# Layer 1's attention: preparation and routing laid out unit by unit, scatters in even units

## The reference

```python
x = x + tanh(g_xattn[0]) * L0_xattn(layernorm(x), ctx)          # 8 heads of 64
x = x + tanh(g_ffn[0])   * L0_ffn(layernorm(x))                 # top 2 of 8, silu(a)*b
x = x + tanh(g_xattn[1]) * L1_xattn(layernorm(x), ctx, ctx)     # 16 heads of 8, biases
x = x + tanh(g_ffn[1])   * L1_ffn(layernorm(x))                 # top 2 of 8, gelu
```

```python
qh, kh, vh = proj(q, Wq, bq), proj(k, Wk, bk), proj(v, Wv, bv)  # (b, 16, rows, 8)
attn = softmax(einsum('bhqd,bhkd->bhqk', qh, kh) / sqrt(8))
out  = einsum('bhqk,bhkd->bhqd', attn, vh)                      # then @ Wo + bo
topk_vals, topk_idx = top_k(tokens @ router_w.T, 2); weights = softmax(topk_vals)
```

## Time and profile before

| what | us |
|---|---|
| median of 3 runs | 858.85 |
| lowest, highest | 857.03, 860.1 |
| profiled execution, its own time | 851.79 |
| its span on the core | 849.8 |

### The profile page before, as it was taken

One profiled execution on the slowest core, in us unless ns is written; L12 is line 12 of the kernel. 1 busy time (PEld: TensorE's weight loads), 2 busy tenths in 40 slices (PEclk: granted clock), 3 DMA queues, 4 the chain that ended last, 5 costly groups with the idle time before them and its releaser, 6 DMA issues.

```text
span 849.8 us, 17654 instructions
## 1 busy us (share of the span) xinstructions
PE 694.9 (82%) x5008; PEld 630.4 (74%) x5008; DVE 569.2 (67%) x2013; ACT 454.3 (53%) x1211; POOL 478.6 (56%) x693
## 2 busy tenths in 40 slices
PE   5899998997997668888879988988788847578688
PEld 4789987887886658777768887777678737567577
DVE  2668877886675555787887877977876725344553
ACT  3467675764555425555656776577476623233333
POOL 4233366664477555685554435667566766655562
PEclk9999999997999879999998999999999989799999
DMA  9334000001102222444633535533433022233445
GB/s 263 113 99 127 1 22 19 25 22 43 33 32 74 64 78 82 120 109 119 168 83 90 115 69 108 118 93 69 123 90 70 25 84 80 85 94 109 133 130 179
DMA packets 89934, 75.74 MB, mean 89 GB/s; under 512 B 28872, under 2 KB 78056, under 8 KB 89776
## 3 DMA queue, kind: packets, MB, share of 16 engines
q1 hardware_dynamic: 72144, 48.96, 23.3%
q0 software_dynamic: 9088, 19.68, 7.2%
q10 hardware_dynamic: 8608, 5.99, 2.5%
HBM read 44.99 MB, written 34.00 MB: 93 GB/s over the span
## 4 chain that ended last, share of the span: by engine, by line
PE 46%; DVE 20%; ACT 13%; issue 9%; another core or an unknown queue 8%; DMA 1%; DVEq 1%; POOL 0%; SPq 0%; POOLq 0%; ACTq 0%
PE banks L1003 8%; PE banks L1022 5%; PE banks L866 5%; PE banks L850 5%; PE banks L742 3%; DVE row_max L1243 3%; PE banks L806 2%; PE banks L744 2%; PE banks L925 2%; PE banks L743 2%; PE banks L830 2%; DVE prob L1246 2%; PE banks L840 2%; DVE hidden L1496 1%
## 5 line engine op out<-in xcount | busy, mean ns | idle before, releaser
L1677 POOL DMA_INDIRECT y_rows<-y_sb,result_at x156 | 152.8, 980 | 114.0 <-DVE result_at L1476 56.5
L1003 PE MATMUL banks<-xb,up 128*128 128x128 f32 x936 | 147.7, 298 | 65.0 <-ACT xb L1186 20.7
L1003 PEld LDWEIGHTS banks<-xb,up 128*128 128x128 f32 x936 | 128.1, 207 | 75.1 <-issue 43.1
L1670 POOL DMA_INDIRECT x_rows<-xm,row x128 | 127.5, 996 | 34.8 <-issue 30.4
L1022 PE MATMUL banks<-down,hidden 128*128 x624 | 104.6, 294 | 15.1 <-DVE y_sb L1513 6.7
L1022 PEld LDWEIGHTS banks<-down,hidden 128*128 128x128 f32 x624 | 89.0, 206 | 20.6 <-issue 20.2
L1632 POOL TENSOR_TENSOR v_flat<-v_raw,row_head 104x64 f32<-104x64 f32 (+1 forms) x128 | 55.9, 462 | 80.6 <-ACT v_raw L1165 80.0
L866 PE MATMUL banks<-v_flat,prob_t 128*128 128x108 f32 (+2 forms) x640 | 85.4, 282 | 6.7 <-ACT prob_t L1149 3.6
L866 PEld LDWEIGHTS banks<-v_flat,prob_t 128*128 128x128 f32 (+1 forms) x640 | 78.8, 195 | 16.0 <-ACT prob_t L1149 8.6
L1203 ACT ACTIVATE gate<-banks,block_bias 128x128 f32<-128x128 f32 x156 | 48.7, 365 | 74.9 <-PE banks L1003 47.8
L1243 DVE TENSOR_REDUCE row_max<-banks 128x8 f32<-128x616 f32 x96 | 75.8, 790 | 16.6 <-PE banks L821 8.9
(11 more groups left out here) (216 smaller groups left out, 1653.9 us busy)
## 6 DMA issues: line engine op xcount, KB each, us to landing
x_norm<-x_rows SPq DMA_DIRECT2D x86, 72.0 KB
x_far<-x_rows SPq DMA_DIRECT2D x70, 72.0 KB
gathered<-y_rows ACTq DMA_DIRECT2D x32, 128.0 KB
q_rows<-up_raw SPq DMA_DIRECT2D x8, 512.0 KB
q_even<-q_rows SPq DMA_DIRECT2D x12, 256.0 KB
q_odd<-q_rows SPq DMA_DIRECT2D x12, 256.0 KB
y_rows<-y_sb,result_at POOLq DMA_INDIRECT x156
k_rows<-up_raw SPq DMA_DIRECT2D x32, 77.0 KB
```

Source lines behind the costliest of these rows:

```text
L1003: done = pe.matmul(banks[:, UP_BANK[i % 2], part * P:(part + 1) * P], block_w[:, i % WR, part // 2, part % 2 * P:(part % 2 + 1) * P], xb[: ...
L1670: pool.indirect_dma_start(out=x_rows[i // HG][:, :], out_offset=bass.IndirectOffsetOnAxis(ap=row[:, n, c:c + 1], axis=0), in_=xm[:, i % 2, ...
L1677: pool.indirect_dma_start(out=y_rows[k][:, :], out_offset=bass.IndirectOffsetOnAxis(ap=result_at[:, i % (2 * YR):i % (2 * YR) + 1], axis=0 ...
```

## The change

Nothing is added or removed: every engine issues the same number of instructions before and after, in another order, in the 64 units of layer 1's attention and the first steps behind them.

- Preparation of group g is laid out by unit: `norm` at 8m+1, `normalize` at 8m+2, `k1` at 8m+4, `xt` at 8m+7, `q1` at 8m+8, `q_load` at 8m+9, `k_load` at 8m+10 to 12 (m = g-2). Before it was `norm` and `k1` at 8m+7, `normalize` at 8m+8, `xt` at 8m+9, `q1` at 8m+10, `q_load` at 8m+11, `k_load` at 8m+10 to 12. Group 2 is a little later than the rule: `normalize` at 4, `k1` at 6.
- Routing: `mnormalize` one unit after `mnorm` (8m+6), not two (8m+7).
- Scatters at offsets 9, 11, 13, 15 (units 8m+6, 0, 2, 4), not 8, 10, 12, 14 (units 8m+5, 7, 1, 3); those of group 5 at 8, 9, 10, 11, one pair of DMAs to a unit. Group 6 and 7 and all of layer 0 keep their tables.

```diff
-    usual, hurried = steps
+    usual = steps[0]
     for g in range(NG):
         u = spacing * g + lag
-        steps = hurried if g == NG - 2 else usual
-        for kind, step in zip(("mnorm", "mnormalize", "mturn", "route", "pick", "rank", "lead"), steps[0]):
+        steps_of = steps[g - NG + 4] if NG - 3 <= g < NG - 1 else usual
+        for kind, step in zip(("mnorm", "mnormalize", "mturn", "route", "pick", "rank", "lead"), steps_of[0]):
...
 def attention1_steps(tasks):
     per = 2 * GS
+    preparation = prepare_attention1()
...
-            ahead = u if u == 0 else u + 1
-            if u == 0 or ahead % per == 0:
-                g = ahead // per + 1
-                pending = prepare_attention1(g) if g < NG else []
...
-            begun = pending.pop(0) if pending else []
+            begun = preparation.get(u, [])
...
-def prepare_attention1(g):
-
-    n = NG + g
-    if g == 1:
-        return [[("norm", n)], [("normalize", n)], [("xt", n)], [("q1", g)], [("q_load", g)]]
-    load = [("k_load", g, piece) for piece in range(6)]
-    return [[("norm", n), ("k1", g)], [("normalize", n)], [("xt", n)], [("q1", g)] + load[0:2], load[2:4] + [("q_load", g)], load[4:6]]
+def prepare_attention1():
...
+    for u, kind in enumerate(("norm", "normalize", "xt")):
+        put(u, (kind, NG + 1))
+    put(3, ("q1", 1))
+    put(4, ("q_load", 1))
+    for g in range(2, NG):
+        u = 2 * GS * (g - 2)
+        put(u + 1, ("norm", NG + g))
+        put(u + (2 if g > 2 else 4), ("normalize", NG + g))
+        put(u + (4 if g > 2 else 6), ("k1", g))
+        put(u + 7, ("xt", NG + g))
+        put(u + 8, ("q1", g))
+        put(u + 9, ("q_load", g))
+        for n in range(3):
+            put(u + 10 + n, ("k_load", g, 2 * n), ("k_load", g, 2 * n + 1))
+    return at
...
-             route_tasks(1, 2 * GS, 13, (((0, 2, 3, 5, 6, 7, 9), (8, 10, 12, 14)), ((0, 1, 2, 3, 4, 5, 6), (6, 6, 7, 7))))]
+             route_tasks(1, 2 * GS, 13, (((0, 1, 3, 5, 6, 7, 9), (9, 11, 13, 15)), ((0, 1, 3, 5, 6, 7, 9), (8, 9, 10, 11)),
+                                         ((0, 1, 2, 3, 4, 5, 6), (6, 6, 7, 7))))]
```

More of the change, by code:

```diff
@@ L118, in route_tasks @@
                     at.setdefault(u + step + 2, []).append(("block_bias", layer, g // HG))
-        for j, step in enumerate(steps[1]):
+        for j, step in enumerate(steps_of[1]):
             at.setdefault(u + step, []).append(("scatter", layer, g, j))
@@ L213, in prepare_attention0_at, with put @@
     return places + [[("norm", g)] if turn == 0 else [("normalize", g)] if turn == 1 else []]
-def prepare_attention1(g):
-    n = NG + g
-    if g == 1:
-        return [[("norm", n)], [("normalize", n)], [("xt", n)], [("q1", g)], [("q_load", g)]]
-    load = [("k_load", g, piece) for piece in range(6)]
-    return [[("norm", n), ("k1", g)], [("normalize", n)], [("xt", n)], [("q1", g)] + load[0:2], load[2:4] + [("q_load", g)], load[4:6]]
+def prepare_attention1():
+    at = {}
+    def put(u, *units):
+        at.setdefault(u, []).extend(units)
+    for u, kind in enumerate(("norm", "normalize", "xt")):
[13 more added lines that the diff above has]
+    return at
 def first_keys_and_queries():
@@ L282, in order @@
     out += first[1:] + [("wvo", 0), ("wvo", 1), ("ctx", 1), ("gates",)]
-    tasks = [route_tasks(0, GS, 6, ((range(7), (5, 6, 7, 8)), ((0, 1, 2, 3, 3, 4, 5), (5, 5, 5, 5)))),
-             route_tasks(1, 2 * GS, 13, (((0, 2, 3, 5, 6, 7, 9), (8, 10, 12, 14)), ((0, 1, 2, 3, 4, 5, 6), (6, 6, 7, 7))))]
+    tasks = [route_tasks(0, GS, 6, ((range(7), (5, 6, 7, 8)), (range(7), (5, 6, 7, 8)), ((0, 1, 2, 3, 3, 4, 5), (5, 5, 5, 5)))),
+             route_tasks(1, 2 * GS, 13, (((0, 1, 3, 5, 6, 7, 9), (9, 11, 13, 15)), ((0, 1, 3, 5, 6, 7, 9), (8, 9, 10, 11)),
+                                         ((0, 1, 2, 3, 4, 5, 6), (6, 6, 7, 7))))]
     after0 = [[("expert", 1, e)] for e in range(NEXP)] + first_keys_and_queries()
```

## The result

| | before | after |
|---|---|---|
| median of ten executions each, us | 859.58 | 854.75 |
| ratio, 95% interval | | 0.9937, 0.9911 to 0.9964 |
| profiled execution, own time / span, us | 851.79 / 849.8 | 853.45 / 851.7 |

Faster, by 5.4 us as the ratio has it (4.8 by the medians), where 12.0 was forecast. The changed kernel was measured four more times beside the kernel before (e5, f4, g4, h2, on three chips): 0.9925, 0.9885, 0.9924, 0.9950. Over all 51 and 99 executions the means are 853.4 and 859.3, so **5.9 us, give or take 1.1**. One execution of the changed kernel (1247 us) and one of the kernel before (868.3 us) were slow and are in neither mean nor ratio.

The account below looks back on a forecast made before the run. No engine is full; ACT's late `xm_t` and `xt` at group starts set the pace. PE idle 24.30 - 4.7 - 5 x 1.65 = 11.35, plus 0.65, gives 12.0 us gained: 846.9 us median, range 841 to 857.

Parts of the forecast that it names:

- the sum: Layer 1's attention: PE's 24.30 us idle in five groups, less 4.7 and 1.65 each, plus 0.65, gives 12.0 us gained.
- the model group: Group with preparation and no routing; its 1.65 us of PE idle was taken as what each of five groups keeps.
- The group with the totals: Group where 4.7 us of PE idle, waits for DVE's tables (2.9 and 1.8), was to stay, besides the 1.65.
- Both are moves between units of one group: `k1` to 8m+4 and `q1` to 8m: charged only with the idle time that the reference group keeps.
- A few tenths: Unit 8m+7: the most lateness expected from ACT's `xm` standing just ahead of the unit that now has `xt`.
- rival 2: The wait only moves: to `xm_t` behind `q1`'s copy, or, second branch, to `xt_l` behind `xm` at 8m+7; 858 us, 10%.
- `k1` in 8m+4, at most 4.4: Unit 8m+4, 3.74 us with the ranks, becomes at most 4.4 with `k1`'s low part on DVE.
- Scatters at nothing: Scatters to even units, apart from POOL's masks in odd units: cost nothing, covered by POOL's idle time.
- SP's queue at nothing: Key reads behind `q_load` are issued by 20 us of a 27 us group; slack goes from 8.5 to 7, cost nothing.
- rival 3: Keys come late behind `q_load` on SP, so PE and DVE wait at group ends; 6.5 us slower, 865 us, 7%.
- rival 4: Scatters hold DVE's combinations in the even units, up to 1.09 us each; 10.9 us back, 857.8 us, 4%.
- Rival 1: DVE becomes the bound, dense from 8m+2 to 8m+5; PE regains only its own stall, 6.6 us, for 852.3 us; 15%.

Follow-up runs that it names:

- e5: The changed kernel itself, run again as control beside e7 on the same chip; 852.80 us, ratio 0.9925 to the kernel before.
- e7: Changed kernel plus four constant statistics instructions on DVE at the end of each unit 8m+3; 862.36 us, ratio 1.0035 to the kernel before.
- e3: Changed kernel with `q1` at 8m+9 and `q_load` at 8m+10, each one unit later; ratio 0.9931 to the kernel before.
- g3: Changed kernel with only the scatters of groups 0 to 5 back at offsets 8, 10, 12, 14; ratio 0.9905 to the kernel before.
- f2: Changed kernel with only `norm` moved, to 8m-1 instead of 8m+1; ratio 0.9902 to the kernel before.
- g1: Changed kernel with `norm` moved to 8m-1, `xt` to 8m+5 and `q1` to 8m+6; ratio 0.9928 to the kernel before.
- h1: Preparation of g1 with the scatter table of g3; 852.09 us, ratio 0.9899 to the kernel before.
- e1: Changed kernel with the routing and scatter tables of before, so only preparation is new; ratio 0.9949 to the kernel before.
- e4: Changed kernel with `xt` of groups 3 to 7 at 8m+6, ahead of ACT's `xm`; ratio 0.9984 to the kernel before.

## Why the forecast was half right

The direction and the place held, and of the mechanism the first half: the two waits at 8m+1 went. What that would give back did not come. The wait for `xm_t` is gone, that for `xt_l` is gone from 8m+1, and the maxima beginning 8m+1 and 8m+2 came 3.7 closer (forecast: some 4). What failed, in the order of the prediction:

- **The step that failed is the sum's "The rest cannot go to zero; the group with preparation alone keeps 1.65, and I take that for each".** Nothing in the rows said that a group with routing could come down to the idle time of one without. Idle time of PE went from 24.30 to 19.04 instead of 12.95, and the model group itself went from 1.65 to 2.76. The group with the totals came out as summed (6.47, against 4.7 + 1.65 = 6.35). The whole miss is in the other four, which kept 12.57 and not 6.60. The price should have been asked unit by unit: how long is DVE's work there, how long PE's. In 8m+3 and 8m+4 the units were already dense, and e7 shows for 8m+3 that DVE's time is paid there nearly in full.
- "Both are moves between units of one group. I charge them with what the reference group leaves idle." `q1` in unit 8m cost 1.64 a group (mean of four). That it writes the bank of `v1` was in the code and not in my working; the output product behind it makes DVE wait. e3 shows that this is not an extra that can be lifted off: without it the time stands in 8m+1.
- "A few tenths" for `xt` behind `xm` at 8m+7: DVE waits 1.80 in unit 23, and the unit takes 3.81 as before. It was rival 2's second branch, in part, and the prediction's own sign (no wait of DVE for `xt_l` over 1 us) failed by it.
- `k1` in 8m+4, at most 4.4: it took 4.19 in unit 28 (545.94 to 550.13), 3.55 to 4.20 in groups 2 to 4. Right. In the group with the totals it went from 4.72 to 5.45 (5.16 in three of the other profiles).
- **Scatters at nothing: wrong.** The six units 8m+3 pay 3.3 us for them, and the length about 2, of which 0.7 to 1.6 stand in units at full clock (g3). I looked at scatters beside combinations, where no hold shows (0.73, and 0.73 after). The cost came in 8m+3, by POOL's masks and bias meeting the selection, which no scatter parts in this unit any more.
- SP's queue at nothing: right. The store of q is issued at 535.55, the last keys at 546.22, done by 549, 18 us into a group of 29, where 20 of 27 was allowed. Rivals 3 and 4 are out.
- **Rival 1, DVE as the bound**, which had 15% and 852.3, describes best what is left in the middle of a group. Its marks are there (8m+3 above 4 us in groups 2 to 7, 8m+4 at 4.2 in two of four), but the third, PE waiting for DVE's subtraction, is hardly new (9.1 us in ten times, 8.8 in nine before). The evidence is e7; f2 speaks against it in 8m+1. That its 852.3 is so near has some luck in it: the 6.6 was the wait for `xm_t` alone, and what came out is a gain in 8m+1 and 8m+2 less what other units took back. I spoke against it with DVE's idle total of a group, which is an average over units that are full and units that are not.

One sum of the chances is off: above 857 stand rival 3's 7, half of rival 2's 10 and rival 4's 4, which make 16% and not 13.

In numbers, by length: the preparation gave 7.5, the routing tables took 1.6 to 2.1, and 5.4 came out; the time says 5.9. Parted by the clock as above, the tables took 0.4 to 1.6. The missing 6 were in no order that I tried: the best one, g1, shortens the length by 3.6 more (0.8 to 2.9 of them in units at full clock), and no gain in time could be told from it. The same holds for h1, whose interval (0.9843 to 0.9954) overlaps that of its control (0.9919 to 0.9981). Both are faster than the kernel before; whether either is faster than the changed one stays open. How much of 8m's 4.65 would go if `q1` had a bank of its own wasn't tried.

## What to carry to other kernels

Price a move of work by the unit that it leaves and the unit that it enters, engine by engine; the idle time of a whole stretch, or of a lighter stretch beside it, is not a floor that the heavier one will reach. A step that needs ACT and then DVE, or that reuses a PSUM bank, should be looked at with everything that stands ahead of it in ACT's queue in the same unit. And to find out where an engine is the bound, put a known dose of work that waits for nothing on it in two places: here 6.9 us cost 9.6 in one and 0.6 in the other, each give or take 2.7. Before two lengths are compared, look at the granted clock of each piece: here 6.3 of a difference of 6.9 us stood in units where one of the two profiles had a lower one.

## What I had not expected of the hardware

- DVE operations on a few bytes took as long as the POOL operation beside them: a cast of 128x8 took 0.61 instead of 0.20.
- In all five profiles of the changed kernel the granted clock is low in units 1 and 2 of group 0 (0.50 to 0.72). In three it stays low into unit 3, which then takes 6.3 to 6.9 us instead of 4.2. PE was busy all through that unit, as these stretches of it show, in the changed kernel's first profile and in e5's. 0.64 is a mean of both levels, 1.2 and 2.4 GHz. Why it stays low in some executions wasn't tried; the length leaves group 0 out for this reason.

```profile
455.10:461.70 6.60, 6.60 (x37) 6.36 (x38) 2.26 (x4) 2.75 (x6) 1.77 (x5) 0.64 0.03 6
```

```profile
457.97:462.17 4.20, 4.10 (x33) 3.92 (x34) 2.26 (x4) 2.61 (x7) 1.70 (x4) 1.00 0.07 24
```

- Behind the attention, from 670 to 700 us, the mean granted clock was 0.91 in g4 and 0.72 in f4, the same kernel; f4's phase behind the attention took 183.0 us, g4's 179.6. That is one source of the scatter between executions, which is as large as what the experiments had to tell apart.
- The chip of e1 to e4 ran the kernel before in 792.8 us, the others in 858 to 860. There is no profile of the same kernel on both, but e4's units 8m+1, 8m+2, 8m+4 and 8m+5, which its edit leaves alone, take the changed kernel's 2.58, 3.55, 3.76 and 2.60. So the attentions seem equally long; the difference stands in the two expert phases, where e3's traffic was 123 GB/s from 250 to 400 us and e5's 97 from 250 to 440.
